# Sums of x's squares on GpSimd for tiles 1 to 3, squares of the output weights on VectorE

## The reference

```
rfs(v)  = 1/32 * exp(xis) * exp(v @ (xis*P).T - 0.5 * sum(v*v) * xis^2)
x1      = layernorm(x + rfs(x) @ rfs(W).T)
h       = silu(x1 @ Wg.T / 127) * (x1 @ Wu.T / 127)        # hidden 3072
out     = layernorm(x1 + h @ Wd.T / 127)
```

## Time and profile before

| what | us |
|---|---|
| time, median of 3 runs (lowest to highest) | 618.03 (617.77 to 620.71) |
| time of the profiled execution | 618.38 |
| span of its slowest core, core 6, from first to last instruction | 616.6 |
| spans of the eight cores | 611.2 to 616.6 |
| TensorE busy on core 6 | 588.8 (95%) |
| VectorE, ScalarE, GpSimd busy on core 6 | 431.0, 189.9, 367.9 |

### The profile page before, as it was taken

The page is one execution under the profiler, slowest core; times in us unless marked ns, Lnnn a source line. Parts: engine busy times, 40 slices in busy tenths (PEclk is TensorE's granted clock), DMA queues, the critical chain, the costliest instruction groups (busy, mean ns, idle before and its releaser), DMA issues.

```text
span 616.6 us, 9077 instructions; the slowest of 8 cores (611.2 to 616.6 us)
## 1 busy us (share of the span) xinstructions
PE 588.8 (95%) x2680; PEld 263.4 (43%) x2680; DVE 431.0 (70%) x697; ACT 189.9 (31%) x358; POOL 367.9 (60%) x336
## 2 busy tenths in 40 slices
PE   3799999999988999999999999999999999999995
PEld 0344444444433444444444444444444444444442
DVE  1369323577999877777777787777777769776775
ACT  0244824454442232223223222322330014400243
POOL 9200999300002276999999999899615495614950
PEclk9889899999999999999999999999999999999998
DMA  8999461599740011223223323223423739863433
GB/s 95 162 172 237 161 215 36 177 296 300 199 103 1 6 64 69 103 95 129 104 93 129 104 94 129 103 94 130 170 104 95 281 116 339 308 261 127 182 137 136
DMA packets 45103, 90.23 MB, mean 146 GB/s; under 512 B 19328, under 2 KB 26496, under 8 KB 41728
## 3 DMA queue, kind: packets, MB, share of 16 engines
q1 hardware_dynamic: 36464, 58.47, 29.0%
q0 software_dynamic: 8448, 30.94, 19.7%
q10 hardware_dynamic: 144, 0.26, 0.1%
HBM read 60.82 MB, written 23.59 MB: 137 GB/s over the span
## 4 chain that ended last, share of the span: by engine, by line
PE 88%; DVE 5%; DMA 3%; issue 2%; ACT 1%; POOL 1%; DVEq 0%; ACTq 0%; POOLq 0%
PE P L576 44%; PE P L869 24%; PE P L315 9%; PE P L467 6%; PE P L349 4%; DMA proj<-projT 3%; DVE z L485 1%; DVE xsum L204 1%; DVE x1t L204 1%; PE P L382 1%; DVE ebuf L595 0%; POOL xf L80 0%; DVE x1k L497 0%; POOL proj L80 0%; DVE wbuf L633 0%
## 5 line engine op out<-in xcount | busy, mean ns | idle before, releaser
L576 PE MATMUL P<-x1t,ring 128*128 128x512 bf16 x768 | 182.1, 379 | 5.4 <-DVE ebuf L595 5.0
L204 POOL TENSOR_TENSOR ring<-ring 128x512 bf16<-128x512 bf16 x120 | 135.2, 1159 | 12.5 <-DMA ring<-wgu 9.0
L576 PE MATMUL P<-xsum,ring 128*128 128x512 bf16 x576 | 140.1, 379 | 0.8 <-DVE xsum L204 0.8
L576 PEld LDWEIGHTS P<-x1t,ring 128*128 128x128 bf16 x768 | 74.8, 98 | 97.2 <-issue 7.7
L637 POOL TENSOR_TENSOR hact<-wbuf,hact 128x512 bf16<-128x512 f32 x24 | 27.8, 1160 | 117.9 <-ACT ebuf L591 70.0
L204 POOL TENSOR_TENSOR stage<-stage 128x512 bf16<-128x512 bf16 x60 | 68.0, 1169 | 44.5 <-DMA stage<-wd 42.6
L576 PEld LDWEIGHTS P<-xsum,ring 128*128 128x128 bf16 x576 | 56.3, 98 | 69.0 <-issue 2.2
L869 PE MATMUL P<-tbuf,hact 128*128 128x512 bf16 x384 | 83.7, 379 | 0.0
L315 PE MATMUL P<-xf,proj 128*128 128x512 bf16 x256 | 65.3, 419 | 14.4 <-DMA proj<-projT 14.4
L869 PE MATMUL P<-tbuf,sbuf 128*128 128x512 bf16 x288 | 62.8, 379 | 0.0
L591 ACT ACTIVATE ebuf<-P 128x512 f32<-128x512 f32 x48 | 28.2, 587 | 101.3 <-PE P L576 101.3
(11 more groups left out here) (85 smaller groups left out, 633.4 us busy)
## 6 DMA issues: line engine op xcount, KB each, us to landing
tbuf<-t_hbm SPq DMA_DIRECT2D x14, 1536.0 KB, 6.9
ring<-wgu POOLq DMA_DIRECT2D x12, 1024.0 KB, 5.2
xtok_sb<-xtok SPq DMA_DIRECT2D x16, 512.0 KB, 4.9
t_hbm<-stage SPq DMA_DIRECT2D x8, 896.0 KB, 4.8
stage<-wd POOLq DMA_DIRECT2D x12, 512.0 KB, 3.7
xf<-xfm POOLq DMA_DIRECT2D x16, 256.0 KB, 24.9
x_hbm<-x1k SPq DMA_DIRECT2D x16, 256.0 KB, 3.6
xres<-x_hbm SPq DMA_DIRECT2D x16, 256.0 KB, 6.3
```

The lines of the kernel that those rows point to most:

```text
L204: out[o] = (p.mark(eng, lambda e: e.tensor_tensor(d, a, b, op), *toks, *behind),)
L576: fn = lambda e, dk=dk, lhsT=lhsT, rhs=rhs: e.matmul(bank(b), lhsT, rhs, start=(start and dk == 0), stop=(stop and dk == 3), skip_group_ch ...
```

## The change

The two additions within the halves and the last addition go to GpSimd for tiles 1, 2 and 3; the squaring stays on VectorE, and so does all of tile 0. The squares of the output weights go from ScalarE to VectorE. The places of the calls in the program do not change.

```diff
     def norm_x(t):
 
+
+        eng = "vector" if t == 0 else "gpsimd"
         o = (t % 2) * 4096
         half = []
         for k in range(2):
@@
-            half.append(p.mark("vector", lambda e, c=o + a: e.tensor_tensor(
+            half.append(p.mark(eng, lambda e, c=o + a: e.tensor_tensor(
                 sqx[:, c:c + 1024], sqx[:, c:c + 1024], sqx[:, c + 1024:c + 2048], OP.add), t_q))
-        t_sq[t] = p.mark("vector", lambda e: e.tensor_tensor(
+        t_sq[t] = p.mark(eng, lambda e: e.tensor_tensor(
             sqx[:, o:o + 1024], sqx[:, o:o + 1024], sqx[:, o + 2048:o + 3072], OP.add), *half)
@@
     def norm_w(k):
         a, b = k * 2048, (k + 1) * 2048
-        t_sq["w", k] = p.mark("scalar", lambda e: e.activation(sqw[:, a:b], iw[:, a:b], AF.Square), ld_iw[k])
+        t_sq["w", k] = p.mark("vector", lambda e: e.tensor_tensor(
+            sqw[:, a:b], iw[:, a:b], iw[:, a:b], OP.mult), ld_iw[k])
```

## The result

The changed kernel takes 624.84 us (median), 1.011 times the kernel before, with a 95% interval from 1.0088 to 1.0131: 5.4 to 8.1 us slower. The profiled execution took 626.79 with a span of 625.3 on its slowest core, now core 1. Lines have moved by two or three: L274, L277 and L279 are the squares and the two kinds of addition, L284 the matmul that wants them, L308 the eviction, L295 the squares of W, L385 the matmuls on these.

What follows compares the result with a forecast made beforehand. TensorE was taken to bound the kernel, gapless in core 6's first stage. Span 616.6 + 2.0 (tile 1) + 4.4 (tile 2) = 623.0, plus 1.8, less 0.35: 624.4 us; own range 623 to 626, with rivals 620.0 to 626.6.

Steps and rivals of the forecast that it cites:

- The sum: Whole kernel: span 616.6 + 2.0 + 4.4 = 623.0 us, median time 624.4 us, 1.0% slower.
- nothing new behind 80 us: Sign of being right: after 80 us in the timeline, no new waits appear.
- Tile 1, 2.0 us: Before tile 1's sums matmul: three GpSimd additions of 2.25 us delay it from 38.76 to 40.8, TensorE idle 2.0 us.
- Tile 2, 4.4 us: Before tile 2's sums matmul: 6.4 us later, 4.4 us more idle TensorE, 2.4 of them tile 3's squares pushing in.
- The turns: Tile 2's sums: VectorE's two squares of tile 3 alternate with GpSimd's additions at SBUF, costing 2.4 us.
- Squares of W on ScalarE, priced at nothing: First stage: taking four squares of 1.85 us off ScalarE gains nothing on core 6, as they don't set TensorE's pace.
- that TensorE set the pace: First stage, core 6: TensorE runs without a gap, so work taken off VectorE, ScalarE or GpSimd can't shorten it.
- Evictions in front of the weights' sums, priced at nothing, at most 1.4: Tile 3's evictions before L382: nothing lost at the clock of before; at full clock TensorE stands up to 1.4 us.
- The rival of the clock, 0.12: Behind tile 2's wait TensorE's clock falls to near 1.2 GHz, 1.3 us more, 625.7 us; chance 0.12.
- Not slower: GpSimd's additions are mostly fixed cost, 1.16 us each, so sums come in time: 618.0 us or slightly less; chance 0.05.
- clock gives back: Tile 3's stretch, at 0.81 before, runs at full clock after idling, returning 2.1 us: 621.4 to 623.7; chance 0.05.

Runs made afterwards that it cites:

- before_again: The kernel before, unchanged, run again on the chip of most follow-up runs; ratio 1.000 to the kernel before.
- after_again: The changed kernel, unchanged, run again on that chip; two runs, 627.3 and 625.4 us against a median of 619.1 for the kernel before.
- sums_only: Against the changed kernel: squares of W back on ScalarE, sums of tiles 1 to 3 still on GpSimd; 1.0089 times the kernel before.
- sums_late3: Against sums_only: norm_x(3) moved behind the evictions of tile 2's first half; 1.0064 times the kernel before.
- sums_act3: Against sums_only: ScalarE instead of VectorE squares tile 3, at the same place; 1.0074 times the kernel before.
- weights_only: Against the changed kernel: all sums of x's squares back on VectorE, squares of W still on VectorE; 0.994 times the kernel before.
- weights23: Against the kernel before: only the squares of the last two quarters of W move to VectorE; ratio 1.000.
- tile2_only: Against the kernel before: only tile 2's sums move to GpSimd; ratio 1.0029.
- tile3_weights: Against the kernel before: tile 3's sums on GpSimd and all squares of W on VectorE; ratio 0.9952.

## Why the prediction was right, and where it was not

**The sum.** 624.4 was forecast, 624.84 came; 6.4 us on the span were worked out, and the ratio says 5.4 to 8.1. The two waits are where they were said to be, with the cause that was given. That the sum is this near is partly luck. On core 6, for which it was worked out, the stage is 6.1 us longer, but made up otherwise: 2.1 up to `norm_x_mm(1)`, 3.2 and not 4.4 from there to `norm_x_mm(2)`, nothing to `norm_x_mm(3)`, and 0.8 behind it, where the forecast had nothing. Core 1, which set the profiled time, lost more: "nothing new behind 80 us" did not hold there, where the wait of 2.21 and the clock behind it cost 4 us together. The profiled execution took 626.79 where 624.8 was worked out for it. Between before_again and after_again the stage grew by 7.5, although the change took the 2.0 us wait for the copy away; evictions (1.3) and the clock behind the second wait (1.2) stand against that.

**Tile 1, 2.0 us.** Measured 2.08 on the slowest core, 1.0 to 3.0 by core. An addition takes 2.11, not 2.25, so about 0.2 of it is fixed (against 1.16 for half the columns). 2.0 was the value at core 6's own clock, at which the stretch from 0 to 1 took 13.5. At full clock it takes 12.5, and TensorE stands for 3.0, as on four cores of after_again; the prediction did not say so.

**Tile 2, 4.4 us.** The term that was sized wrong. The idle time was 3.28 on core 6, 3.1 to 4.3 over the result's cores and mostly 4.75 in sums_only and after_again. From one matmul to the next it is 19.1 us on core 6, where the prediction's times give 20.3 (40.8 to 61.1). The turns were predicted instruction by instruction: the squares of tile 3 took 4.89 for both and the last addition 2.91. sums_late3 and sums_act3 show that they cost 1.8 us and not 2.4. The prediction charged each square its whole 1.22. Rows 4 had the smaller figure already: VectorE's addition that waited until 187.29 was through at 187.85, 0.56 later and not 0.68. A further 0.4 is three additions of 2.11 instead of 2.25.

**Squares of W on ScalarE, priced at nothing.** This is the step that was wrong in kind. The prediction read rows 8 and set them aside as not being of the slowest core. But core 6 of the kernel before has the same queue on ScalarE, squares right in front of the copy:

```profile
68.76 3.69 ACT L293 ACTIVATE sqw<-iw 128x2048 bf16<-128x2048 bf16 x2
72.36 0.57 ACT L287 ACTIVATE sbc<-P 128x512 f32<-128x512 f32 x1
```

It was covered only because TensorE, at 0.81 of its clock, reached that point late (71.11). before_again shows 2.02 us on every core, and weights_only is worth 0.6%. I had named the cover (that TensorE set the pace) and not what it costs when it goes. It did the forecast no harm, since in the result's execution of the kernel before five of eight cores had no such wait.

**Evictions in front of the weights' sums, priced at nothing, at most 1.4.** Measured 0 to 2.2. Turns are not kept with every instruction of GpSimd. In the changed kernel on core 1:

```profile
74.24 5.25 DVE L295 TENSOR_TENSOR sqw<-iw 128x2048 bf16<-128x2048 bf16 x1
```

```profile
74.06 0.93 POOL L80 DMA_DIRECT2D t_hbm<-stage  x1 [0.59 <-POOL stage L204]
74.88 5.61 POOL L204 TENSOR_TENSOR stage<-stage 128x512 bf16<-128x512 bf16 x4
```

The square was asked for at 74.24 and, by its own 1.22, ran from 78.3. Before it came the issue of a store and three sums of 1.16, to 78.36. I had one sum per square. Core 4 of weights23 shows the same once more: a square asked for at 69.3, during a store's issue (68.87 to 69.80), took 5.01 us, through the issue and three sums from 69.69.

**The rival of the clock, 0.12.** It came true on six of the eight cores, the slowest among them, behind waits of 3.12 to 4.30 us, and on tile2_only's eight cores behind 4.32. In tile2_only the stretch behind takes 15.8 to 17.0 instead of 14.24, so 1.6 to 2.7 us, more than the 1.3 that I gave it. On the other two cores of the changed kernel, 2 and 3, it did not, behind 3.06 and 3.23 (14.25 and 14.24). It deserved a larger chance. On core 6 it cost nothing net: the stretch takes 16.47 where it took 16.43 before, at 0.81. "TensorE: Matmul & The Clock Gate" of the Trainium skill, in its table of the two states, has the fall follow an idle stretch. These rows bear that out: 0.50 stands behind the 4.30.

**Not slower, clock gives back.** The first did not come. The second came on cores 2 and 3 only: their stretch from 2 to 3 ran at full clock, 14.25 and 14.24 where it had been 15.08 and 15.43, and they don't set the time. In before_again the stretches at 0.81 are missing, so there was nothing to give back.

What stays open: why tile3_weights is not as fast as its parts; why the store on GpSimd's queue breaks the turns; and a part of the 3.7 us of weights_only, since 2.2 us of its shorter stage lie in 3 to W, where the wait for the copy was, and 0.3 in 2 to 3, while 0.4 lies in 0 to 1, ahead of what was changed.

## What to carry to other kernels

Work moved off a busy engine to an idle one is still late if the idle one is slower and a consumer has little slack: write the slack behind each result (here 2.5 us) beside the added time (8.7 us from the first square to the last sum instead of 4.7), and look for instructions that share the port with it before counting on the overlap. Where a core's slower clock covers a queue, read the wait on the faster cores as what the kernel costs at full clock. Test the parts of a change apart: here one half of it, and a single tile of the other, are each 0.6 to 0.75% faster than the kernel before, and the whole is 1.1% slower.

## What the runs showed of the hardware that was not expected

VectorE and GpSimd exclude each other at SBUF where both read two operands, and mostly in turns; a turn costs GpSimd less than VectorE's whole instruction (0.8 to 1.0 us for a square of 1.22). But VectorE's square waited 4.0 us through a store's issue and three sums in a row, and a second time in weights23. A GpSimd addition of 128x1024 in bf16 takes 2.11 us, against 1.16 for 128x512. After 4.3 us of idle time in a dense stretch TensorE's clock was at 1.2 GHz on all cores of tile2_only; in the changed kernel it was so on six cores behind 3.12 to 4.30 us, and not on two behind 3.06 and 3.23. The length of the wait alone does not tell: on core 3 of the changed kernel the clock was at 0.50 behind tile 1's wait of 1.86 us and at 1.00 behind tile 2's of 3.23, and in before_again it fell on one core of eight behind the same 2.02.
